# Leaving the blocks above the diagonal out of a chunked scan on one Trainium2 core

## The reference, cut to what matters

```python
def step(state, inp):
    x_t, b_t, c_t, dt_t = inp
    decay = jnp.exp(dt_t * a)[..., None, None]
    b_bar = dt_t[..., None] * b_t
    state = decay * state + b_bar[..., None] * x_t[:, :, None, :]
    y_t = jnp.einsum('bhn,bhnp->bhp', c_t, state)
    return (state, y_t)
```

## Time and profile before

| | |
|---|---|
| median of 3 runs | 1397.62 us (1397.34 to 1399.22) |
| profiled execution, its own time | 1401.03 us |
| span of that execution | 1399.3 us |
| PE busy | 1335.8 us (95%) |
| DVE, ACT, POOL busy | 945.3, 685.8, 351.8 us |
| mean granted TensorE clock | 0.985 |

### The profile page before, as it was taken

The page is one execution under the profiler, slowest core; times in us unless marked ns, Lnnn a source line. Parts: engine busy times, 40 slices in busy tenths (PEclk is TensorE's granted clock), DMA queues, the critical chain, the costliest instruction groups (busy, mean ns, idle before and its releaser), DMA issues.

```text
span 1399.3 us, 26836 instructions
## 1 busy us (share of the span) xinstructions
PE 1335.8 (95%) x10517; PEld 827.2 (59%) x10531; DVE 945.3 (68%) x2649; ACT 685.8 (49%) x1351; POOL 351.8 (25%) x452
## 2 busy tenths in 40 slices
PE   8999999999999999999999999999999997999984
PEld 4447655586457665586456764576555863567543
DVE  2424797487874787567974878747875779746782
ACT  3534653754546562556436454466526554463312
POOL 3005301171105401072012611053010630134110
PEclk9999999999999999999999999999999998999997
DMA  8100001020000200020010200011000200101010
GB/s 278 45 0 32 9 23 49 1 82 31 27 23 8 75 31 27 23 81 18 14 49 1 82 31 27 23 33 50 30 27 23 81 24 8 49 3 50 31 49 4
DMA packets 47565, 54.47 MB, mean 39 GB/s; under 512 B 7624, under 2 KB 42312, under 8 KB 47440
## 3 DMA queue, kind: packets, MB, share of 16 engines
q1 hardware_dynamic: 41424, 46.41, 9.8%
q0 software_dynamic: 6016, 6.35, 1.7%
HBM read 34.84 MB, written 17.85 MB: 38 GB/s over the span
## 4 chain that ended last, share of the span: by engine, by line
PE 86%; DVE 6%; issue 4%; ACT 1%; DMA 1%; POOL 1%; POOLq 0%; DVEq 0%
PE ps L1576 46%; PE ps L1758 8%; PE ps L1655 4%; PE ps L1701 3%; PE ps L1898 2%; PE ps L1908 2%; PE ps L1667 2%; PE ps L1645 2%; PE ps L1716 1%; PE ps L1673 1%; PE ps L1863 1%; PE ps L1829 1%; PE ps L1684 1%; PE ps L1564 1%; PE ps L1594 1%
## 5 line engine op out<-in xcount | busy, mean ns | idle before, releaser
L1576 PE MATMUL ps<-xT,wb_s 128*128 128x512 f32 x512 | 233.7, 603 | 4.5 <-ACT xT L740 4.4
L1576 PE MATMUL ps<-xT,wc_s 128*128 128x512 f32 x512 | 225.4, 593 | 0.0
L1576 PEld LDWEIGHTS ps<-xT,wc_s 128*128 128x128 f32 x512 | 96.1, 190 | 112.3 <-issue 111.9
L1576 PEld LDWEIGHTS ps<-xT,wb_s 128*128 128x128 f32 x512 | 94.4, 192 | 114.4 <-issue 105.7
L1065 DVE SCALAR_TENSOR_TENSOR xT<-xc,cols_s,xT 128x512 f32<-128x512 f32 x192 | 134.8, 748 | 2.7
L1576 PE MATMUL ps<-hT,wx_s 128*128 128x512 f32 x256 | 117.6, 603 | 0.0
L1576 PE MATMUL ps<-hT,wz_s 128*128 128x512 f32 x256 | 113.8, 598 | 0.1
L1758 PE MATMUL ps<-CT,xT 128*128 128x256 f32 x512 | 111.9, 379 | 0.9 <-DVE xT L1239 0.9
L765 ACT ACTIVATE BT<-ps 128x512 f32<-128x512 f32 x64 | 37.9, 593 | 151.3 <-PE ps L1576 151.3
L1758 PEld LDWEIGHTS ps<-CT,xT 128*128 128x128 f32 x512 | 97.2, 190 | 17.8 <-issue 5.0
L1153 DVE TENSOR_TENSOR Mt<-ps,Eg 128x512 f32<-128x512 f32 x128 | 82.2, 684 | 26.5 <-PE ps L1701 26.5
(11 more groups left out here) (298 smaller groups left out, 2572.4 us busy)
## 6 DMA issues: line engine op xcount, KB each, us to landing
xr<-x SPq DMA_DIRECT2D x8, 1024.0 KB, 10.1
x_scratch<-xr SPq DMA_DIRECT2D x32, 256.0 KB, 2.1
out<-EC SPq DMA_DIRECT2D x32, 256.0 KB, 2.1
BT<-x SPq DMA_DIRECT2D x7, 1024.0 KB, 5.8
modrow<-mod_scratch SPq DMA_DIRECT2D x8, 512.0 KB, 7.0
w_s<-w SPq DMA_DIRECT2D x2, 1024.0 KB, 11.2
BT<-x SPq DMA_DIRECT2D x2, 512.0 KB, 5.4
xT<-wmod SPq DMA_DIRECT2D x1, 1024.0 KB, 9.7
```

Source lines behind the costliest of these rows:

```text
L1576: ins = t_.matmul(bank[:, :], w[:, k, m * P:(m + 1) * P], rhs[:, k, half * HALF:(half + 1) * HALF], start=k == 0, stop=k == nk - 1)
```

## The change

Only the three 64x64 blocks on and below the diagonal are computed. Two head tiles make a pair (PAIR = 192 columns): 128 columns (LONG) for keys of one half and all queries, 64 columns for keys of the other half and the later queries. For even tiles the long part's keys sit on partitions 0 to 63; for odd tiles the halves of the tokens are swapped, so that the long part sits on partitions 64 to 127. That needs swapped copies of B, of the decay rows, of dt and of the tokens (`xsw`, in spare columns of `Mt`).

On PE, intra becomes `intra_long` and `intra_short`, each on 64 rows of keys, with a wait of PE for its own inter and for its own long part (both write the same places). The mask on the diagonal (`diagonal`) is issued separately for the two banks, and the second half moves behind `intra_long`; the scores come in two pairs with inter between them. Exp and the mask products work on 384 of 512 columns. ACT makes the swapped tokens (`swap`). On DVE, `y_stats(0, 0, 4)` stands behind `skip(6)` instead of ahead of `state(6)`. The diff, without the removed lines of functions shown above:

```diff
         def sb(name, shape, dt=F32):
+
+            return t[:, 0:2 * PAIR].rearrange("p (a n) -> p a n", a=2)
...
         gT = XB[:, 1, :, :].rearrange("p a b -> p (a b)").rearrange("p (t n) -> p t n", t=FT)
...
+                    if m < KC and m % 2:
+                        src = halves(proj.bank(q)[:, :].rearrange("p (c n) -> p c n", c=4))
+                        dst = halves(BT[:, half, m, :].rearrange("p (c n) -> p c n", c=4))
+                        for e in range(2):
+                            ins = a.activation(dst[:, :, e, :], src[:, :, 1 - e, :], ACT.Copy)
...
+                    if k % 2:
+                        for e in range(2):
+                            ins = a.activation(dst[:, :, e, :], src[:, :, 1 - e, :], ACT.Copy,
+                                               scale=headsel[:, k:k + 1])
...
-                        a.activation(Eg[:, s * HALF:(s + 1) * HALF], ps[s][:, :], ACT.Exp
+                        a.activation(Eg[:, s * HALF:s * HALF + 2 * PAIR], ps[s][:, 0:2 * PAIR], ACT.Exp
...
+                def swap(c):
+
+                    if c >= 2:
+                        act.wait_ge(xt_filled, at(xt_filled, b, c - 1))
+                    elif later(b):
+                        act.wait_ge(xt_filled, at(xt_filled, b - 1, T))
+                    src = halves(xT[:, 1::2, c * P:(c + 1) * P])
+                    dst = halves(xsw[:, c % 2, :, :])
+                    for e in range(2):
+                        ins = a.activation(dst[:, :, e, :], src[:, :, 1 - e, :], ACT.Copy)
+                    ins.then_inc(swapped_ready, 1)
...
+                swap(0)
+                swap(1)
                 decay(0)
                 tokens(0)
                 for c in range(1, T):
                     if c == T - 1 and not last:
                         ln_apply(b + 1, 0)
                     tokens(c)
+                    if c < T - 1:
+                        swap(c + 1)
...
+                for e in range(2):
+                    ins = v.tensor_scalar(dst[:, :, e, :], src[:, :, 1 - e, :], bdt_s[:, :], None, ALU.add)
...
+                        o = s * HALF
+                        v.tensor_tensor(Mt[:, c % 2, o:o + 2 * PAIR], ps[2 + s][:, 0:2 * PAIR],
+                                        Eg[:, o:o + 2 * PAIR], ALU.mult).then_inc(Mt_ready, 1)
...
-                    if c == 6:
-                        y_stats(0, 0, 4)
                     if c < T - 1:
                         state(c)
                     else:
                         y_stats(1, 4, 7)
                     skip(c)
+                    if c == 6:
+                        y_stats(0, 0, 4)
                 y_stats(2, 7, 8)
...
+                for e in range(2):
+                    for i in range(2):
+                        o = e * 2 * P + i * P
+                        ins = t_.transpose(proj.bank(J_UT)[:, o:o + P], (uqx if e else uq)[:, i * P:(i + 1) * P],
+                                           ident[:, :])
...
+                for e, sums in enumerate((upto, upto_x)):
+                    t_.matmul(bank[:, 0:64].rearrange("p (c e s) -> p c e s", e=2, s=2)[:, :, e, :], sums[:, :],
+                              da.rearrange("p (c e s) -> p c e s", e=2, s=2)[:, :, e, :], start=True, stop=True)
...
+                    ins.then_inc(inter_filled, 1)
...
+            def intra_long(b, c):
                 pe.wait_ge(Xd_ready, at(Xd_ready, b, c + 1))
                 pe.wait_ge(Mt_ready, at(Mt_ready, b, 2 * c + 2))
+                if c:
+                    pe.wait_ge(inter_filled, at(inter_filled, b, c))
                 for h in range(HEADS):
                     k, hh = h // 2, h % 2
+                    rows, o = half(k % 2), (hh + k) % 2 * HALF + k // 2 * PAIR
+                    ins = t_.matmul(y_tile(k, half(hh)), XB[rows, c % 2, 0, h * STATE:(h + 1) * STATE],
+                                    Mt[rows, c % 2, o:o + LONG], start=c == 0 and k < 2, stop=True,
+                                    skip_group_check=c > 0 or k >= 2)
...
+
+            def intra_short(b, c):
+
+                pe.wait_ge(long_filled, at(long_filled, b, c + 1))
+                for h in range(HEADS):
+                    k, hh = h // 2, h % 2
+                    rows, o = half(1 - k % 2), (hh + k) % 2 * HALF + k // 2 * PAIR
+                    ins = t_.matmul(y_tile(k, half(hh))[:, 64:128], XB[rows, c % 2, 0, h * STATE:(h + 1) * STATE],
+                                    Mt[rows, c % 2, o + LONG:o + PAIR], start=False, stop=True,
+                                    skip_group_check=True)
...
+
+            def last_output(b):
+
+                inter(b, T - 1)
+                intra_long(b, T - 1)
...
+                    pe.wait_ge(swapped_ready, at(swapped_ready, b, c + 1))
...
+                        ins = t_.transpose(ps[6][:, k * P:(k + 1) * P], xsw[:, c % 2, k // 2, :] if k % 2 else xT[:, k, c * P:(c + 1) * P],
+                                           ident[:, :])
                     ins.then_inc(xt_filled, 1)
...
+                            pe.wait_ge(Eg_ready, at(Eg_ready, b, 2 * (c - 1) + r + 1 if c else 0))
+                        q = half(r)
+                        for e in range(2):
+                            t_.matmul(by_pair(ps[r])[half(e), :, 0:LONG], Lw[q, c * P + 64 * e:c * P + 64 * e + 64],
+                                      R8[q, e::2, c * P:(c + 1) * P], start=True, stop=True)
...
+                        for e in range(2):
+                            t_.matmul(by_pair(ps[r])[half(1 - e), :, LONG:PAIR],
+                                      Lw[q, c * P + 64 * (1 - e):c * P + 64 * (1 - e) + 64],
+                                      R8[q, e::2, c * P + 64:(c + 1) * P], start=False, stop=True,
+                                      skip_group_check=True)
+
+                def diagonal(c, r):
+
+                    for d in range(2):
+                        out = ps[r][half(d), 0:2 * PAIR].rearrange("p (a t n) -> p a t n", a=2, t=3)[:, :, 0::2, :]
+                        ins = t_.matmul(out, identb[half(r), half(r)],
+                                        causal[half(r), :, half(r)].rearrange("p (a t) n -> p a t n", a=2),
+                                        start=False, stop=True, skip_group_check=True)
+                    ins.then_inc(cd_filled, 1)
+
+                def scores(c, pair):
...
+                    o, w = chunk(c).start, pair * PAIR
+                    for k in (2 * pair, 2 * pair + 1):
+                        for r in range(2):
+                            t_.matmul(ps[2 + r][half(k % 2), w:w + LONG], BT[half(r), c // 4, k, o + 64 * (k % 2):o + 64 * (k % 2) + 64],
+                                      CT[half(r), c // 4, k, chunk(c)], start=True, stop=True)
+                    for k in (2 * pair, 2 * pair + 1):
+                        for r in range(2):
+                            ins = t_.matmul(ps[2 + r][half(1 - k % 2), w + LONG:w + PAIR],
+                                            BT[half(r), c // 4, k, o + 64 * (1 - k % 2):o + 64 * (1 - k % 2) + 64],
+                                            CT[half(r), c // 4, k, o + 64:o + P], start=True, stop=True)
                             if k == KC - 1:
...
                 for c in range(T - 1):
                     turn(c + 1)
                     cumdiff(c + 1)
-                    scores(c + 1)
+                    diagonal(c + 1, 0)
+                    norm = c == T - 2 and not last
+                    if norm:
+                        diagonal(c + 1, 1)
+                    scores(c + 1, 0)
                     inter(b, c)
-                    if c == T - 2 and not last:
+                    scores(c + 1, 1)
+                    intra_long(b, c)
+                    if norm:
                         ln_in(b + 1, 0)
-                    intra(b, c)
+                    else:
+                        diagonal(c + 1, 1)
+                    intra_short(b, c)
                     state(c)
...
```

More of the change, by code:

```diff
@@ L111, in sb, with halves, by_pair, half @@
             return ctx.enter_context(nc.sbuf_tensor(name, shape, dt))
+        PAIR, LONG = 192, 128
+        def halves(ap):
+            return ap.rearrange("p k (a n) -> p k a n", a=2)
+        def by_pair(t):
+            return t[:, 0:2 * PAIR].rearrange("p (a n) -> p a n", a=2)
+        def half(e):
+            return slice(64 * e, 64 * e + 64)
         def y_tile(k, rows=slice(0, P)):
@@ L535, in _ @@
                                  base=0, pattern=[[1, P]], channel_multiplier=-1))
+            link(g.tensor_copy(upto_x[:, :], upto[:, :]))
+            link(g.memset(upto_x[64:128, 0:64], 1.0))
+            link(g.memset(upto_x[0:64, 64:128], 0.0))
             link(g.memset(hsum, 0.0))
@@ L548, in _ @@
                     link(g.memset(src[:, :, 64 * half + first:64 * half + first + ROWS], value))
-            for half in range(2):
-                block = slice(64 * half + 2 * ROWS, 64 * half + 2 * ROWS + NG)
-                link(g.memset(Lsrc[64:128, :, block], 1.0))
```

(24 more changed lines are left out.)

63 lines of the change are left out of this document (31 added, 32 removed).

## The result

The changed kernel takes 1427.94 us (median of 5, 1424.37 to 1432.65) against 1397.62: a ratio of 1.0218, interval 1.0196 to 1.0239. The forecast of 1410 had the sign right, but the loss is 30 us and not 12, and the time lies above the range of 1399 to 1422.

What follows compares the result with a forecast made beforehand. TensorE, busy 95% of the span, was taken as the bound. Faster PE work (-1.0) and new waits for DVE (+3.4) gave +16.8 us over batches 0 to 6, batch 7 -4.1: +12.7, forecast 1410 us, range 1399 to 1422.

Steps and rivals of the forecast that it cites:

- Queue of a plain chunk: PE's pieces from differences to state in one scan chunk: 2.48 us instead of 2.69, 0.21 less.
- self-wait: PE waiting for its own records: 0.38 us, covered behind inter by scores; behind intra_long 0.16 lost after the mask's cover.
- rival 1: Diagonal mask halves run free beside other row half: 0.11 us less a chunk, 1406; chance 0.60 together with the forecast.
- rival 3: 64-column groups cost as much as 128-column ones, 0.109 us: about +0.4 a chunk, 1425; chance 0.06.
- The loop that decides: Inter waits for DVE's skip sums, delayed by the second mask half: 1.1, 0.9, 2.0 in chunks 3-5, +3.4 us a batch.
- Rival 4: DVE's loop does not bind, PE's savings stand alone: -11, 1387; chance 0.15 below, 0.08 about even.
- The first wait: Chunk 3, statistics held by the 1 MB load: skip sums 8.3 us after the scores, PE after 7.2, wait 1.1.
- A regular scan: Scan of batches 0 to 6, chunk gains against waits for skip sums: +12.0 us over the seven scans.
- Outside the scans: Extra PE work per batch: dt transposes and small product 0.44 us, uncovered last chunk output 0.25.
- Last output: The last chunk's output stands outside the scan without cover: 0.2 to 0.25 us more per batch.
- Batch 7: Last batch, no norm statistics: wait falls from 2.96 to 1.2 us, half clock after it may vanish; sum -4.1.
- rival 2: PE's new idle waits bring 3 us at half clock in each batch: 10 us more, 1421; chance 0.11.

Runs made afterwards that it cites:

- the load experiments: Two of three mid-scan loads (residual, modulation rows) issued only after the last chunk's scores: changed kernel 1415.66 us, kernel before 1394.33 us.
- The mask edit: Changed kernel with the second diagonal mask always beside the first, ahead of the scores: 1414.34 us, ratio 1.0116 to the kernel before.
- the statistics edit: Changed kernel with the next batch's norm statistics of chunks 4 and 5 moved into DVE's idle stretches: 1404.90 us, ratio 1.0051 to the kernel before.
- the faster version with the same rows: Changed kernel, masks ahead, statistics in gaps, loads later; short intra records on the long ones' rows, no wait for long part (wrong result): 1386.51 us.
- the version with the scores together: Changed kernel with masks ahead, statistics in gaps and loads later, plus both score pieces of a chunk ahead of inter: 1407.88 us.

## Why the prediction was right in sign and short in size

**The step that failed** is the sum, which went from PE's queue and DVE's loop alone and had two terms at nothing. PE's instruction supply was not in it at all: by the load experiments it is 12.3 - 3.0 = 9 of the 30 us between the medians, in part through the clock. The half clock behind the waits was kept as a rival at 11 in 100: it cost 6 us in the profiled execution. Outside the scans the sum was short by another 3.4. The parts that the sum did price add up to what was forecast within a scan (+1.8 against +1.7), though by two errors that cancel, which is luck.

- **Queue of a plain chunk: wrong in size.** Forecast -0.21, measured 4.21 - 4.27 = -0.06. Differences 0.19 (0.18). The masks and the self-wait together 0.25 (0.38): the first half costs nothing, since the scores start in the other tiles beside it (786.49 twice), so rival 1 is half true. Scores and inter 1.24 (1.11), intra_long 0.50 (0.44), short part and switch 0.39 (0.37), state 0.61 (0.56). The term that was missing: a piece that follows another with the same tile shape but other rows or columns also exposes up to 0.08 us of its first group, and the change made six pieces of a chunk into twelve. That reading is argued from the rows, and they are uneven: long to short scores lose 0.01, short scores to intra_long 0.08; no run tested it by itself. The short records themselves cost what was forecast (0.93 for 16 groups of 64 columns, measured above); rival 3 falls.
- **Self-wait: right in kind.** 0.29 uncovered, row change included (forecast 0.38 less the group's 0.11 = 0.27).
- **The loop that decides: right in two waits of three.** Inter waits 0.78 and 1.87 where the forecast had 0.9 and 2.0, but 0.16 to 0.17 (once 0.64) where it had 1.1. The mask edit took away half of these waits, the statistics edit nearly all. Rival 4 falls. The first wait was a small difference of long times: the load's way was right (in batch 2, 8.3 us from the scores to inter), but PE came by after 7.6 us and not 7.2, for its chunks are slower than forecast.
- **A regular scan:** +1.8 us (35.7 - 33.9, without half clock or stalls), forecast +1.7. Two errors cancel, by luck: 0.8 less gained in the chunks, 0.7 less lost to the waits.
- **Outside the scans: too low.** dt 0.44, exact. Last output +0.37 instead of 0.25. Further 0 to 0.6 a batch that I had at nothing: x projections that wait 0.2 for ACT, and in some batches the softmax's transposes, 0.36 late. Mean 1.17 against 0.69, 3.4 us in seven batches.
- **Batch 7: right.** The wait fell to 1.19 (forecast 1.2) and the half clock behind it did not come; -3.1 behind the last scan (forecast -2.6). Part of that is where half clock falls further on, which differs between executions.
- **Clock, rival 2: came in four of seven batches**, 6 us in the profiled execution. I had it at 11 in 100 as all or nothing; it is a chance per wait. With the loads later the same wait was followed by it in two batches of seven. The slower executions of the changed kernel have the lower mean clock, which fits, but they have no profile.
- **PE's instruction supply: not in the forecast at all.** It is the largest of the missing terms, the 9 us above. I had read four "issue" stalls of the kernel before as noise, and counted PE's cost in columns alone.

## What to carry to other kernels

Leaving work out in small blocks is paid in instructions, pieces and waits of an engine for itself; price each piece by its start-to-start distance, not by its columns. Before asking for a faster engine, look at who stands between its input and its buffer: moving a few statistics into the idle stretches of DVE, busy for 66% of the span, gained 23 us. And look at what large loads run beside the stretch with the most instructions per us: holding two loads back by one wait made both kernels faster, the kernel before by a little only (ratio 0.9973 to 0.9998). Before leaving work out, give the full version the same repairs: with them the blocks left out gained nothing that could be measured.

## What the runs showed of the hardware

- PE stalls for 0.2 to 2.7 us in its instruction supply when 2.6 MB of loads run beside a stretch of small matmuls: 3.4 us in all with 192 matmul and weight-load records a chunk, 7.3 with 232, 13.1 with 256, none with 192 or 232 when 1.5 MB of the loads come later (but up to 2.5 us at a time in the faster version with the same rows). In the kernel before and the changed one the instruction packet starts 7.5 to 10.5 us after its forerunner, and PE resumes 1.2 to 1.5 us after it has landed.
- Matmuls in different tiles pass each other. At 786.84 two records of inter start ahead of the last two records of the scores (786.87), which stand ahead of them in the program. The Trainium skill (TensorE: Matmul & The Clock Gate, "What overlaps and what doesn't") says that matmuls are strictly in order in start and end; this trace does not agree for the starts where tiles differ.
- Groups of four records of 64 f32 columns cost 0.058 us, 64 records 0.93. By the floor of about 25 ns between starts that the Trainium skill states (same page, "Wait — 56ns, not 53.3ns?") the 64 would take 1.6 us, an estimate, so the floor doesn't hold between tiles.
- An idle of 1.87 us was followed by 3.4 us at level 0.50 in four of seven like places (two of seven with the loads later), one of 1.13 in none of seven. One of 1.19 in the last batch was followed by it in the version with the scores together, and in none of the changed kernel's other versions.
